# A two-layer block of recurrence, attention and experts: sums of expert pairs moved from GpSimd to VectorE, with new tables of sequence

## The reference

```python
def reference(x, ...):                       # x: (4, 1024, 128) float32
    xn = layernorm(x)
    x = x + L0_attn(xn) + L0_ffn(xn)
    xn = layernorm(x)
    return x + L1_attn(xn) + L1_ffn(xn)

# L0_attn: a gated recurrence of 4 heads (key size 16, value size 32)
#   S = exp(w_t)[..., None] * S + k_t v_t^T ;  o_t = r_t (S + u k_t v_t^T)
#   then a norm of each head's output, * silu(g), @ W_o
# L0_ffn: every token is cut into 8 heads of 16; 16 experts of 64 hidden units
t = (x @ Wm + bm).reshape(tokens * 8, 16)
w = softmax(t @ expert_emb); topw, topi = top_k(w, 2)
hmid = gelu(einsum('td,edi->tei', t, W1) + b1)        # all 16 experts
eo = einsum('tei,eio->teo', hmid, W2) + b2
out = sum over the 2 chosen experts of topw * eo, then @ Wo + bo
# L1_attn: causal attention, 16 query heads of 8, one shared key and value head
# L1_ffn: two rounds of rmsnorm, router (8 experts, top 2), swiglu experts (256)
```

## Time and profile before

| | us |
|---|---|
| median of 3 runs | 1273.62 |
| lowest, highest | 1271.74, 1275.04 |
| the profiled execution, its own time | 1275.04 |
| span of the profiled execution | 1273.7 |
| TensorE busy in the span | 1187.4 (93%) |
| VectorE busy | 1048.3 (82%) |
| ScalarE busy | 881.5 (69%) |
| GpSimd busy | 488.4 (38%) |
| mean granted TensorE clock | 0.976 of 2.4 GHz |

### The profile page before, as it was taken

The page is one execution under the profiler, slowest core; times in us unless marked ns, Lnnn a source line. Parts: engine busy times, 40 slices in busy tenths (PEclk is TensorE's granted clock), DMA queues, the critical chain, the costliest instruction groups (busy, mean ns, idle before and its releaser), DMA issues.

```text
span 1273.7 us, 28619 instructions
## 1 busy us (share of the span) xinstructions
PE 1187.4 (93%) x11270; PEld 604.5 (47%) x11270; DVE 1048.3 (82%) x1954; ACT 881.5 (69%) x1243; POOL 488.4 (38%) x446
## 2 busy tenths in 40 slices
PE   6889999999998999798999999998999999999977
PEld 3333433334442324465655555555656555555434
DVE  4699779979999885689979898687987898888734
ACT  3588998988798889262366675665766577666666
POOL 3544344374436664420345503555035550000242
PEclk8799999999999999799999999999999999999988
DMA  7433334323232442347654544545434444224111
GB/s 217 131 129 120 108 96 137 101 74 113 94 126 67 142 140 100 99 127 201 191 172 124 172 115 134 163 133 142 109 118 148 119 116 126 76 74 130 32 34 55
DMA packets 129877, 152.97 MB, mean 120 GB/s; under 512 B 16048, under 2 KB 90800, under 8 KB 129616
## 3 DMA queue, kind: packets, MB, share of 16 engines
q1 hardware_dynamic: 111104, 127.50, 33.3%
q0 software_dynamic: 8192, 16.79, 4.6%
q10 hardware_dynamic: 10448, 6.85, 1.8%
HBM read 109.27 MB, written 41.81 MB: 119 GB/s over the span
## 4 chain that ended last, share of the span: by engine, by line
PE 52%; DVE 13%; ACT 4%; issue 3%; DMA 1%; another core or an unknown queue 1%; SPq 0%; DVEq 0%; ACTq 0%
PE ax_sums L2915 9%; PE second_pair L2952 5%; PE second_pair L2807 5%; PE first_pair L495 3%; PE first_pair L483 3%; PE second_pair L3246 2%; PE second_bank L3230 2%; DVE am_top L2853 2%; PE second_bank L3214 2%; ACT ax_prob L2976 2%; PE second_pair L3230 2%; PE second_pair L3214 2%; PE second_bank L3246 2%; PE second_pair L2929 2%; PE second_pair L2825 2%
## 5 line engine op out<-in xcount | busy, mean ns | idle before, releaser
L2976 ACT ACTIVATE ax_prob<-second_pair 128x1024 f32<-128x1024 f32 (+1 forms) x320 | 291.5, 941 | 128.4 <-PE second_pair L2929 64.9
L529 ACT ACTIVATE m_act_h<-first_pair,const 128x1024 f32<-128x1024 f32 x256 | 273.3, 1115 | 47.9 <-PE first_pair L483 39.3
L2853 DVE TENSOR_REDUCE am_top<-second_pair 128x2 f32<-128x1024 f32 (+1 forms) x192 | 222.4, 1175 | 29.0 <-PE second_pair L2807 11.2
L3138 POOL DMA_INDIRECT m_back<-slot_results,mr_slots x128 | 125.5, 980 | 255.4 <-PE second_pair L2952 154.6
L3108 POOL DMA_INDIRECT slot_tokens<-xn,mr_slots x128 | 125.0, 977 | 238.2 <-PE second_pair L3214 104.1
L2915 PE MATMUL ax_sums<-ax_prob,al_vs 128*32 128x512 f32 (+3 forms) x1536 | 155.9, 500 | 5.6 <-ACT ax_prob L2976 4.0
L483 PE MATMUL first_pair<-m_terms,w1s 96*128 96x512 bf16 x512 | 143.5, 387 | 2.7 <-ACT m_act_h L529 2.1
L495 PE MATMUL first_pair<-m_act_h,const 128*32 128x512 f32 x1024 | 129.0, 607 | 7.5 <-DVE m_both L544 2.6
L585 POOL TENSOR_TENSOR m_both<-m_prod,m_both 128x512 f32<-128x512 f32 x64 | 86.2, 1358 | 108.2 <-DVE m_both L544 108.0
L2952 PE MATMUL second_pair<-al_qs,al_ks 51*128 51x512 bf16 (+3 forms) x768 | 113.9, 333 | 10.5 <-ACT ax_prob L2976 4.5
L2807 PE MATMUL second_pair<-al_ks,al_qs 48*128 48x512 bf16 (+3 forms) x768 | 112.8, 329 | 8.6 <-DVE am_top L2853 2.9
(11 more groups left out here) (402 smaller groups left out, 2556.0 us busy)
## 6 DMA issues: line engine op xcount, KB each, us to landing
m_wt<-in_experts SPq DMA_DIRECT2D x96, 384.0 KB
m_share<-shares SPq DMA_DIRECT2D x128, 256.0 KB
m_rows<-slot_tokens SPq DMA_DIRECT2D x60, 128.0 KB
slot_results<-m_y SPq DMA_DIRECT2D x60, 128.0 KB
stack<-mp_part SPq DMA_DIRECT2D x48, 128.0 KB
m_terms<-stack SPq DMA_DIRECT2D x64, 96.0 KB, 4.2
qstack<-ap_qpart SPq DMA_DIRECT2D x48, 128.0 KB
al_qs<-qstack SPq DMA_DIRECT2D x32, 192.0 KB
```

The lines of the kernel that those rows point to most:

```text
L529: A.activation(self.act_h[:, slot, :, :], banks.bank("up", n, ep)[:, :, :], ACT.Gelu, bias=self.w("b1", 4 * half + ep, 4 * half + ep + 1)) ...
L2853: V.tensor_reduce(into[:, 2 * a:2 * a + 2, at], tile[:, :, 0:n], AX, ALU.max, negate=True).then_inc(*banks.empties("max", i, m))
L2976: A.activation(dst, src, ACT.Exp, scale=SCALE).then_inc(*banks.empties("sum", i, u))
L3138: G.indirect_dma_start(self.back[q % 2][:, n, m, :], None, self.results[ph], bass.IndirectOffsetOnAxis(ap=self.route.slots[g][n][:, c * NC ...
```

## The change

The 64 additions of pairs run on VectorE and no longer on GpSimd. They wait for the same product as before, and what reads them is the same. On VectorE the instructions of a level of the recurrence, which came in groups of two or three to a turn, have a turn each, so that other work may come between any two; the same holds for the three GpSimd instructions of an entry scale. The planner has a new price: after a rest of TensorE of over 1.6 its matmuls count double for 5.5. All strings of both tables are new, for both layers and all five engines. No instruction's shape changes, no arithmetic, and no buffer.

```diff
# class Moe0: the sum of a pair goes from gpsimd() to vector_pair()
-    def gpsimd(self):
-        G, g = self.k.nc.gpsimd, self.k.pool
+    def vector_pair(self):
+        V, v = self.k.nc.vector, self.k.dve
         for p in range(PAIRS_OF_UNITS):
             for j in range(2):
                 yield FIRST["pair", p, j]
-                g.wait_ge(*self.banks.done("down", 2 * p + 1, j))
+                v.wait_ge(*self.banks.done("down", 2 * p + 1, j))
                 both = self.product(p, 1, j)
-                G.tensor_tensor(both[:, :], self.prod[j][:, :], both[:, :], ALU.add).then_inc(self.folded, 1)
+                V.tensor_tensor(both[:, :], self.prod[j][:, :], both[:, :], ALU.add).then_inc(self.folded, 1)
# class Recurrence, vector_scales(): a turn for each instruction
                 if h > 2:
-                    yield FIRST["factors", it, h]
-                    self.level(it, h)
+                    for part, name in enumerate(("before", "behind", "factors")):
+                        yield FIRST[name, it, h]
+                        self.level(it, h, (part,))
                 for x in range(NH):
-                    if x == 2:
-                        yield FIRST["scale", it, h, 1]
+                    if x:
+                        yield FIRST["scale", it, h, x]
-                    yield FIRST["scale", it, h, 2]
+                    yield FIRST["scale", it, h, NH]
-            yield FIRST["qk", it]
+            yield FIRST["level", it]
             self.level(it, CH)
+            yield FIRST["qp", it]
...
+            yield FIRST["qk", it]
# class Entry, gpsimd(): the three instructions of a scale in turns of their own
-            yield FIRST["scale", c]
-            self.k.pool.wait_ge(loaded, 16)
-            self.scale(c)
+            for part in range(self.SCALES):
+                yield FIRST["scaled", c, part]
+                self.k.pool.wait_ge(loaded, 16)
+                self.scale(c, part)
# planner
+REST, COLD = 1.6, 5.5
...
+            if engine == "PE":
+                if start - engine_free.get(engine, 0.0) > REST:
+                    cold = start + COLD
+                if start < cold:
+                    takes *= 2
...
-                pool("pair", ("pair", pair, j), at + DOWN_AFTER, 1.26, ("product", n, j))
+                dve("pair", ("pair", pair, j), at + DOWN_AFTER, 0.63, ("product", n, j), port=True)
# FIRST_ORDERS and SECOND_ORDERS: every string is another; the first row of PE's
-        "aaffffgahghhiccgcccibgacckcjcgdddccjcdcjccddcckcdccdcjcckdccdekaccddcckcbcdccddccdckccakccddeccddclaecclkkccddcclcllcffddccmffcabcgcddecchhc"
+        "aaffffgahghhicgccccibcgackjcjcddgccdcdccjcdccddcckcdcckccddkcejaccbadcdckccdcdccdcdcckckccddceccddckclklccddcceaffcclddllcfcfmcgcbaccddecchh"
# program: the streams merged on VectorE and on GpSimd
-            merge(prep.vector(), moe0.vector(), moe0.vector_fold(), ...
+            merge(prep.vector(), moe0.vector(), moe0.vector_pair(), moe0.vector_fold(), ...
-            merge(prep.gpsimd(), prep.gpsimd_weights(), rw.gpsimd(), rw.gpsimd_mixtures(), moe0.gpsimd(), entry.gpsimd(loaded["const2"]), experts.gpsimd_first(), ordered=True)
+            merge(prep.gpsimd(), prep.gpsimd_weights(), rw.gpsimd(), rw.gpsimd_mixtures(), entry.gpsimd(loaded["const2"]), experts.gpsimd_first(), ordered=True)
```

171 lines of the change are left out of this document (93 added, 78 removed).

## The result

The changed kernel takes 1302.80 us (4 runs, 1300.94 to 1306.43), the kernel before 1272.68 beside it (4 runs, 1268.88 to 1275.04): ratio 1.0243, interval 1.0209 to 1.0277. It is 30 us slower. I had forecast 1267, with a range up to 1283.

A forecast was written before the change was run, and what follows sets the result against it. TensorE bounds the program, in turns with VectorE in layer 0. Terms 0 - 3 - 1 - 3 + 0 = -7 took the profiled 1275.0 to 1268.0; less 1.4 to the median, 1266.6, near 1267. Own range 1262 to 1271, wide range 1256 to 1283.

The forecast's parts named there:

- the step on GpSimd in part 1: Layer 0, GpSimd: the 64 sums leaving it free 81.5 us nobody waits for, worth nothing by itself.
- part 1: Layer 0, the 64 sums moved from GpSimd to VectorE: term 0, ends +8 and -4.
- the price on VectorE: Layer 0: each sum 684 ns on VectorE, 43.8 us more for the 64.
- The relief: Layer 0: VectorE's two-input SBUF instructions, less blocked by GpSimd, get 12 us back, 4.2 to 15.
- the term 0: Layer 0: the sums cost no time, VectorE busy 425.6 of 440 us, 97%, if the table spreads it.
- the rival on the slower side: VectorE becomes the bound in its full stretches of layer 0: +10 us, 1280.6; chance 0.25.
- Part 2: Layer 0, TensorE's gaps behind a VectorE blocked by GpSimd shrink: -3 us, ends 0 and -6.
- Part 3: ScalarE: three table loads fewer, 3.8 us, mostly hidden: -1 us, 0 to -3.8.
- Part 4: End of layer 0, 500 to 530 us: TensorE's rest filled, less low clock: -3 us, 0 to -7.
- Part 5: Layer 1, same instructions in another order: term 0, -4 to +4, from a tenth of its idle time.
- my -7: Whole kernel: sum of the five parts, 0 - 3 - 1 - 3 + 0 us, on the profiled execution.

The follow-up runs named there:

- a_noscat3: Changed kernel without the 32 early scatters of layer 0, on a slow chip: 1276.70 us, ratio 0.9993 to the kernel before.
- after_again3: The changed kernel itself run again, nothing altered, on a slow chip: 1304.87 us, ratio 1.0232 to the kernel before.
- a_paced3: Changed kernel with early scatters 2.9 us apart, each waiting for TensorE's count of filled banks, on a slow chip: 1282.88 us, ratio 1.0060 to the kernel before.
- a_best3: Changed kernel with scatters 2.9 us apart, one late mixture earlier, its own banks, layer 1's tables from before; slow chip: 1266.48 us, ratio 0.9935 to the kernel before.
- a_pairs_pool: Changed kernel with the 64 sums back on GpSimd under the new tables, banks kept, on a quick chip: 1263.79 us, ratio 1.0172 to the kernel before.

## Why the prediction was wrong

**What failed is the step on GpSimd in part 1**: "Nobody waits for that time; ... its relief is worth nothing by itself." The relief was not worth nothing: on slow chips it cost 28 us. It took away what parted the scatters, and with long runs of them TensorE's signals come late. I looked at what each sum cost on its queue, and not at what stands next to it there, which the order of GpSimd would have shown ahead: L3108 ran at most six times on end before, thirteen after. The price, by a_noscat3 against after_again3: 28.2 us, of which spacing gives back 22 (a_paced3), or 25 with the banks kept and one mixture earlier (35.0 of a_best3 less 9.8 for layer 1's tables). This is measured on slow chips; quick ones show no late signals. The scatters are in no term and no rival of mine.

**Part 1, the price on VectorE:** 684 ns foretold, 681 measured. The relief was mis-sized: I took 12 us. VectorE's busy time from 40 us to the end of layer 0, before and in the changed kernel:

```profile
40.00:527.00 487.00, 457.29 (x4446) 179.77 (x4444) 418.32 (x802) 404.48 (x462) 240.52 (x196) 0.97 0.33 106
```

```profile
40.00:540.00 500.00, 462.24 (x4448) 176.67 (x4449) 427.55 (x870) 401.83 (x461) 155.01 (x132) 0.96 0.32 104
```

It rose by 9.2 us net of 44.4 for L585, so 35 came back (2 us of layer 1 are in the second row). The tables don't make this: counted up to the last L863, VectorE's time is 417.8 us before, 419.5 with the new tables and the sums on GpSimd (a_pairs_pool), and 426.0 in the changed kernel. L1131 alone gave 10.5 where I had counted 4.2: the share of L585 in GpSimd's time (36%) was no measure of its share in the blocking. VectorE was not the bound, and the term 0 stands: it was 95% busy up to 350 us (275.30 of 290) while TensorE idled 4.2. With that the rival on the slower side fell too; it had the sign and the wrong cause. The Trainium skill's sentence (Perfetto Trace Analysis, Optimizing Scalar/DVE Operations) that a shared port may eat what moving work between those two engines brings was the half that held: here the relief paid 35 of the 44 us that moving it back cost.

**Part 2, TensorE's gaps:** right in sign, too small. TensorE's idle time from 60 to 350 us fell by 10.8, I took 3 with 6 as the end. With the sums on GpSimd and the new tables it had fallen by 7.6 already (a_pairs_pool), so the tables won most of it, not the locks that I had priced. From 60 to 500 us, the stretch that I had named, it rose from 22.4 to 31.1: the stalls lie in it.

**Part 3:** ScalarE's loads fell by three as the order showed (from 30 to 27 in the trace of layer 0). Their worth wasn't tried by itself.

**Part 4, the end of layer 0:** from the last gelu to the last L863 it is 20.8 us before, 13.0 in the changed kernel and 13.0 in a_best3: -7.8, where I took -3 and had -7 as the end. Not all of it is gain, since the new order has more gelus in that place. The clock there rose as I had it: 0.94 from 512 to 542 us, where it was 0.83 from 500 to 530.

**Part 5, layer 1:** I took 0 (-4 to +4); it is +9.8 (1.0057 to 1.0124). The bounds, a tenth of the idle time, had no row behind them: an order can lose by new waits what no idle time of the old one limits. This is the second term that failed.

The sum: on one slow chip the changed kernel without scatters is at +1.1. With +9.8 for layer 1, taken from another chip, -8.7 are left for layer 0; that is a remainder, and the traces bear it out roughly (layer 0 ends at 516.0 us in a_noscat3, 526.4 and 523.8 before; behind it 761.5 against 747.3 and 748.1). With scatters it is +29.3. Had I had the two missing terms, 28.2 and 9.8, my -7 would have made 1305. That my -7 comes so near is luck in its parts: the measures of parts 2 and 4, -10.8 and -7.8, add up to far more than the -8.7.

## What to carry to other kernels

When work leaves a queue, print what then stands side by side on it: a cheap instruction may have been keeping two expensive ones apart. Indirect DMAs of GpSimd were better issued some us apart here, and if a semaphore of another engine's progress paces them, keep what others wait for from standing behind that wait. And time a new table for each layer by itself: here the loss of one hid the gain of the other.
